# Inverse transform along h in a four-layer spectral kernel: products split by the parity of the frequency

## The reference

```python
x: (2, 64, 64, 384) float32; 8 blocks of 48 channels
# layers 0, 2 and 3 (scale of the transforms differs)
xf = rfft2(x, axes=(1, 2))                        # h, w -> 64 x 33 frequencies
o1r = relu(xr @ w1[0] - xi @ w1[1] + b1[0])       # block diagonal, 48 x 48
o1i = relu(xi @ w1[0] + xr @ w1[1] + b1[1])
o2r = o1r @ w2[0] - o1i @ w2[1] + b2[0]
o2i = o1i @ w2[0] + o1r @ w2[1] + b2[1]
x = irfft2(softshrink(o2r) + 1j * softshrink(o2i)) + x
# layer 1: the same with a Hartley transform over b, h, w and c,
# and mixes of the transform and the flipped input
x = dht(softshrink(mix(dht(x), flip(x)))) / size + x
```

## Time and profile before

| | |
|---|---|
| median of 3 runs | 995.19 us (990.65 to 997.57) |
| the profiled execution | 993.3 us, span 991.3 us |
| TensorE busy | 916.0 us, 92% |
| VectorE busy | 577.1 us, 58% |
| ScalarE busy | 475.8 us, 48% |
| granted clock of TensorE, mean | 0.976 |
| traffic of DMAs | 184.41 MB, mean 186 GB/s |

### The profile page before, as it was taken

One profiled execution on the slowest core, in us unless ns is written; L12 is line 12 of the kernel. 1 busy time (PEld: TensorE's weight loads), 2 busy tenths in 40 slices (PEclk: granted clock), 3 DMA queues, 4 the chain that ended last, 5 costly groups with the idle time before them and its releaser, 6 DMA issues.

```text
span 991.3 us, 14302 instructions
## 1 busy us (share of the span) xinstructions
PE 916.0 (92%) x5168; PEld 460.3 (46%) x5168; DVE 577.1 (58%) x869; ACT 475.8 (48%) x757; POOL 81.1 (8%) x157
## 2 busy tenths in 40 slices
PE   2799999999999988999999999999999999999933
PEld 1555555665676655444444434444444444444411
DVE  1255555455454765787775676666666666666511
ACT  2455444444545424434343445565655656666521
POOL 3011111011111110000000101000000000000001
PEclk8899999999999999999999999999999999999986
DMA  9879699469648979856143443343654474554463
GB/s 283 324 206 298 202 282 366 150 180 283 248 136 269 260 237 277 210 138 164 48 114 95 112 127 108 108 123 113 213 170 129 153 247 134 161 156 153 142 192 128
DMA packets 95703, 184.41 MB, mean 186 GB/s; under 512 B 13007, under 2 KB 73769, under 8 KB 93842
## 3 DMA queue, kind: packets, MB, share of 16 engines
q1 hardware_dynamic: 85490, 143.65, 48.0%
q0 software_dynamic: 9696, 39.56, 12.4%
q10 hardware_dynamic: 448, 0.30, 0.1%
HBM read 104.32 MB, written 79.14 MB: 185 GB/s over the span
## 4 chain that ended last, share of the span: by engine, by line
PE 82%; DMA 9%; SPq 2%; DVE 2%; ACT 2%; issue 1%; POOL 0%; ACTq 0%; DVEq 0%
PE psum L948 17%; PE psum L957 16%; PE psum L987 8%; PE psum L1041 6%; PE psum L1065 6%; PE psum L1025 6%; DMA RG<-rows_along_h 6%; PE psum L936 5%; PE psum L967 5%; PE psum L998 4%; PE psum L1052 3%; PE psum L913 3%; PE psum L1014 2%; DMA rows_along_h<-RD 1%; SPq L611 1%
## 5 line engine op out<-in xcount | busy, mean ns | idle before, releaser
L1374 DVE SCALAR_TENSOR_TENSOR RA<-psum,RA 112x896 f32<-112x896 f32 (+1 forms) x120 | 124.1, 1035 | 206.3 <-ACT RA L1222 205.9
L1222 ACT ACTIVATE RA<-psum,small 112x896 f32<-112x896 f32 (+1 forms) x120 | 115.7, 964 | 94.7 <-PE psum L957 94.7
L957 PE MATMUL psum<-RA,RW 112*64 112x448 f32 (+1 forms) x640 | 131.1, 531 | 1.4 <-ACT RA L1213 1.4
L1213 ACT ACTIVATE RA<-psum,RW 112x448 f32<-112x448 f32 (+1 forms) x160 | 89.2, 609 | 80.0 <-PE psum L948 80.0
L1334 DVE COPY RD<-psum 128x672 f32<-128x672 f32 (+2 forms) x122 | 69.5, 571 | 58.3 <-PE psum L987 56.8
L987 PE MATMUL psum<-RD,const 128*128 128x384 f32 (+1 forms) x304 | 98.3, 445 | 3.7 <-DVE RD L1334 2.7
L1207 ACT ACTIVATE RA<-psum 128x384 f32<-128x384 f32 (+2 forms) x72 | 50.6, 702 | 78.9 <-PE psum L936 52.6
L936 PE MATMUL psum<-const,RX 128*112 128x128 f32 x528 | 68.5, 282 | 17.1 <-DMA RX<-rows_along_w 17.1
L1359 DVE TENSOR_TENSOR RX<-RX,RA 112x768 f32<-112x768 f32 (+2 forms) x80 | 80.8, 1011 | 2.5
L1207 ACT ACTIVATE RD<-psum 128x384 f32<-128x384 f32 (+2 forms) x122 | 64.0, 525 | 32.9 <-PE psum L987 30.9
L936 PEld LDWEIGHTS psum<-const,RX 128*112 128x112 f32 x528 | 61.2, 180 | 35.7 <-issue 34.9
(11 more groups left out here) (103 smaller groups left out, 1070.1 us busy)
## 6 DMA issues: line engine op xcount, KB each, us to landing
RG<-rows_along_h SPq DMA_DIRECT2D x7, 3072.0 KB, 11.5
RX<-x SPq DMA_DIRECT2D x16, 768.0 KB, 8.6
rows_along_w<-RX SPq DMA_DIRECT2D x54, 224.0 KB, 5.1
rows_along_h<-RD SPq DMA_DIRECT2D x84, 144.0 KB, 3.3
rows_along_h<-RD SPq DMA_DIRECT2D x56, 168.0 KB, 2.9
out<-RA POOLq DMA_DIRECT2D x12, 768.0 KB, 4.0
RX<-rows_along_w SPq DMA_DIRECT2D x12, 672.0 KB, 6.5
spectrum<-RA POOLq DMA_DIRECT2D x48, 168.0 KB, 4.7
```

Of the source, the lines that this page charges most:

```text
L957: mm = nc.tensor.matmul(bank[b * HALF:(b + 1) * HALF, a * BANK:a * BANK + nk * H], w4[layer][0:ROWS, g, b, a], hidden(slot)[0:ROWS, b * N: ...
L1213: done = nc.scalar.activation(hidden(slot)[0:ROWS, b * N:b * N + nk * H], banks(key)[0:ROWS, b, 0:nk * H], ACT.Relu, bias=bias[layer][0:RO ...
L1222: nc.scalar.activation(dst, src, ACT.Relu, bias=minus_lambda_l0 if key[0] == "S4" else minus_lambda).then_inc(act_emptied, 1)
L1374: nc.vector.scalar_tensor_tensor(out=dst, in0=src, scalar=LAMBDA / 64 if key[0] == "S4" else LAMBDA, in1=dst, op0=ALU.add, op1=ALU.min).th ...
```

## The change

The rows of the h frequencies are held by parity in all tables and modes: 32 even frequencies first, then 32 odd. In `s5` each parity is a product of its own, with 64 rows and 64 output partitions (32 values of h, real and imaginary part), and the columns of a group are taken in two sets of four, one for each half of the output partitions (`set_columns`). So a unit is up to four products of 64x64. Bank 0 holds the even part, bank 1 the odd part. ScalarE copies the odd part to a new tile `odd_part`; VectorE waits for that and writes even + odd (h below 32) and even - odd (h from 32) to `turned`. A group's store is eight DMAs in place of four. In the last two groups ScalarE issues half of the stores, and the load of group 3 of the last pass comes one round later, behind the store of the last group. The rest follows from the order of rows: the views of the mixes, adds and folds have blocks of 32 in place of 64, and the output is stored in contiguous halves.

```diff
+SET = 4
-def bank_columns(e, part, half):
-    c0, c1 = columns_of(e)
-    lo, hi = ((0, 4), (4, c1 - c0))[part]
-    mid = lo + (hi - lo + 1) // 2
-    return ((lo, mid), (mid, hi))[half]
+def set_columns(e, part, half):
+    lo, hi = columns_of(e)
+    first = SET * half + 2 * part
+    return first, min(first + 2, SET * (half + 1), hi - lo)
...
+    by_parity = np.concatenate([a * H + np.arange(e, H, 2) for e in range(2) for a in range(2)])
...
+        odd_part = sb("odd_part", 2 * PASS_C)
...
             def store_turned(e):
                 lo, hi = columns_of(e)
-                for x in range(4):
-                    sp.dma_start(rows_along_h[group_of(e)[0], x, lo:hi].rearrange("k h c -> h k c"),
-                                 turned(e)[x * HP:(x + 1) * HP]).then_inc(turned_stored[e % TURN_SLOTS], 16)
+                for half in range(2):
+                    cols = range(lo + SET * half, min(lo + SET * (half + 1), hi))
+                    for x in range(4):
+                        sp.dma_start(rows_along_h[group_of(e)[0], x, cols.start:cols.stop].rearrange("k h c -> h k c"),
+                                     turned_rows(e, half, x % 2)[:, x // 2, 0:len(cols)]
+                                     ).then_inc(turned_stored[e % TURN_SLOTS], 16)
...
-                        store_spread(ALL_GROUPS + e, range(4) if e < ALL_GROUPS - 1 else range(2))
+                        for a in range(2 if e < ALL_GROUPS - 2 else 1):
+                            for j in range(2):
+                                for dst, src in spread_stores(ALL_GROUPS + e, a, j):
+                                    sp.dma_start(dst, src).then_inc(turned_stored[(ALL_GROUPS + e) % TURN_SLOTS], 16)
...
                 for q in range(PASS_GROUPS - 1):
-                    if r == min(10 * (PASSES - 1) + 7 + 2 * q, C_ROUNDS - 1):
+                    if r == (10 * (PASSES - 1) + 7 + 2 * q if q < PASS_GROUPS - 2 else C_ROUNDS - 1):
                         load_spread(LAST_PASS + q)
...
-                src = src.rearrange("p (k a h) -> p k a h", a=2, h=H)
+                src = src.rearrange("p (k a h) -> p k a h", a=2, h=HP)
...
+                d = D(first + e)
+                packed = e % PASS_GROUPS == 0
                 for half in range(2):
-                    lo, hi = bank_columns(e, part, half)
...
+                    lo, hi = set_columns(e, part, half)
+                    for parity in range(2):
+                        rows = slice(parity * HALF, (parity + 1) * HALF)
+                        dst = bank[half * HALF:(half + 1) * HALF, parity * BANK:parity * BANK + (hi - lo) * PASS_C
+                                   ].rearrange("p (k c) -> p k c", c=PASS_C)
+                        if packed and lo == 0:
+                            nc.tensor.matmul(dst[:, 0], matrix[rows, HALF:2 * HALF], d[rows, 0], start=True, stop=False)
+                            nc.tensor.matmul(dst[:, 0], matrix[rows, 2 * HALF:3 * HALF], d[rows, 1], start=False, stop=True)
+                            mm = nc.tensor.matmul(dst[:, 1:], matrix[rows, 0:HALF], d[rows, 2:hi + 1], start=True, stop=True)
+                        elif hi > lo:
+                            mm = nc.tensor.matmul(dst, matrix[rows, 0:HALF], d[rows, lo + packed:hi + packed],
+                                                  start=True, stop=True)
...
+        def wait_odd_part_free(eng, key):
+            stage, e, part = key
+            if part == 1:
+                eng.wait_ge(vec_emptied, plan.vec[stage, e, 0])
+            elif e > 0:
+                eng.wait_ge(vec_emptied, plan.vec[stage, e - 1, 1])
...
-                    wait_turn_free(act, at + key[1])
+                    wait_odd_part_free(act, key)
                     wait_filled(act, key)
-                    copy(*s5_views(key, 0, at)).then_inc(act_emptied, 1)
+                    _, _, odd, room = s5_views(key, at)
+                    copy(room, odd).then_inc(act_emptied, 1)
+                    if e >= 2 * ALL_GROUPS - 2 and key[2] == 1:
                         for part in range(2):
+                            act.wait_ge(vec_emptied, plan.vec["5C", key[1], part])
+                        for j in range(2):
+                            for dst, src in spread_stores(e, 1, j):
+                                act.dma_start(dst, src).then_inc(turned_stored[e % TURN_SLOTS], 16)
...
-                nc.vector.tensor_tensor(zr[:, :, 1:H], re[:, :, 1:H], re[:, :, H - 1:0:-1], ALU.add)
-                nc.vector.tensor_tensor(zi[:, :, 1:H], im[:, :, 1:H], im[:, :, H - 1:0:-1], ALU.subtract)
+                nc.vector.tensor_tensor(zr[:, :, 1:HP], re[:, 0, :, 1:HP], re[:, 0, :, HP - 1:0:-1], ALU.add)
+                nc.vector.tensor_tensor(zi[:, :, 1:HP], im[:, 0, :, 1:HP], im[:, 0, :, HP - 1:0:-1], ALU.subtract)
+                nc.vector.tensor_tensor(zr_odd, re[:, 1], re[:, 1, :, ::-1], ALU.add)
+                nc.vector.tensor_tensor(zi_odd, im[:, 1], im[:, 1, :, ::-1], ALU.subtract)
...
-                    wait_filled(vec, key)
-                    copy(*s5_views(key, 1, at)).then_inc(vec_emptied, 1)
+                    vec.wait_ge(act_emptied, plan.act[key])
+                    dst, even, _, odd = s5_views(key, at)
+                    nc.vector.tensor_tensor(dst[0], even, odd, ALU.add)
+                    nc.vector.tensor_tensor(dst[1], even, odd, ALU.subtract).then_inc(vec_emptied, 1)
```

101 lines of the change are left out of this document (46 added, 55 removed).

## The result

The changed kernel takes 999.96 us (median of 20 runs, 993.44 to 1005.99) and the kernel before 995.09 us (20 runs, 990.65 to 1002.37): ratio 1.0038, 95% interval 1.002 to 1.0056. The forecast was 972 us (963 to 984). The profiled execution took 997.33 us, its span is 995.5 us and its mean granted clock 0.954 (before: 991.3 us and 0.976).

What follows compares the result with a forecast made beforehand. TensorE was taken to bound the kernel (82% of the chain of waits). Savings of 26.1 - 2.4 - 1.4 - 1.0 + 2.1 = 23.4 us from 995.2 gave 971.8, rounded to 972 us (range 963 to 984).

Steps and rivals of the forecast that it cites:

- TensorE's products: The `s5` products, 80 units: from 100.8 to 74.7 us over 8 passes, so TensorE saves 26.1 us.
- Quartets and pairs: `s5` units of four or two 64x64 products: 0.80 us for four, 0.82 taken for two, start to start.
- The packed unit: `s5` unit with three 192-column products and one of 384 per parity: from 1.82 to 2.08 us, dearer by 0.26.
- Rival A: `s5`: array quarters work apart in the unit of mixed widths too (1.12 us), small charges halved: 962 us; chance 0.13.
- Evictions and folds (2.4): VectorE's second shrink of a round comes late in some 8 rounds with a fold, 0.3 us each: 2.4 us (0 to 5).
- rival B: `s5` evictions: ScalarE's copy, then two VectorE operations hold PSUM and set the pace; 19.8 us go: 992 us; chance 0.12.
- Short blocks: Operands of mixes and adds in blocks of 32 instead of 64 elements: cost taken as 0.
- Rival D: Mixes and adds: blocks of 32 cost TensorE or VectorE 5%: 982 us; chance 0.11.
- Transfers and SP's queue: Stores go from 4 to 8 issues: 1.4 us returned as first-stage gather wait, 1 us for SP elsewhere (0 to 10).
- Rival C: SP's queue, first stage: extra issues at 4.0 us each make loads and stores late, 45 us left over: 1015; chance 0.06.
- The end: Last load behind the stores gains 4.1 us, ScalarE's store issues give 2.0 back: net gain 2.1 us (-2 to 4).

Runs made afterwards that it cites:

- the change with three mends: Changed kernel with four stores a group, constant products thrown away ahead of five gathers, and group 18's stores left to SP: 976.76 us, 0.9821.

## Why the prediction was wrong

**TensorE's products: right, and too low.** Quartets and pairs take 0.79 to 0.81 us as said. The packed unit takes 1.55 us, not 2.08: the row of the second parity's first product stands at 707.86, ahead of the third of the first parity (708.18). My value took a product to start only behind the start of the one ahead, and here one starts 0.32 us before it; the measured unit lies between that and my 1.12 for quarters that are wholly apart. By the same sum the saving is 100.8 - 8 x (1.55 + 0.82 + 4 x 0.80 + 2 x 1.62) = 30.3 us; I had 26.1. Rival A had a part of the mechanism, and its price was lost with the rest. The two rules that I weighed, of the Trainium skill, TensorEngine Tiling (Array Packing), Key Properties (independent tiles), and of the Trainium skill, TensorE: Matmul & The Clock Gate, Part 3, The mechanism (products start and end in program order), would give 1.12 and 2.08 us; the trace agrees with neither. The starts at 707.86 and 708.18 are not in program order.

**Evictions and folds (2.4): not refuted.** VectorE's idle time ahead of the shrink went from 2.74 to 1.73 us, and over the whole kernel its idle time ahead of shrinks from 205.9 to 132.7: room was used, none ran out. VectorE's busy time rose by 48.5 us (577.1 to 625.6); I had 44 or more in the sum, 50 to 60 as a sign. (the earlier trace rows show 554 ns for the form that I priced at 548, which is 1 us over the 160 operations.) TensorE's list of waits names no shrink, and its longest wait for an eviction outside the end is 3.2 us where the kernel before has 2.7. The eviction's form alone cost 0 to 6 us in the kernel before. By the two together rival B falls; what of the 2.4 us was spent isn't resolved.

**Short blocks: 0, as taken.** The mixes cost the same (1.76 and 1.55 us for units of 448 and 384 columns, as in the earlier trace rows), and so do VectorE's adds (1092 and 958 ns for 896 and 768 columns in both kernels) and its shrinks (1089 and 955 ns, before 1088 and 954). Rival D falls.

**Transfers and SP's queue: the step that failed.** I wrote that the load "is issued by its round and lasts a fixed time" and charged 1.4 us there and 1 us elsewhere, up to 10. Measured by the number of issues, it is 13 us. The fixed time was right, or nearly: the first gather landed 15.4 us behind its issue before and 14.4 after, the third 11.8 and 11.0. What was wrong is the issue, and that I looked at one gather only. The load isn't issued when TensorE reaches its round. SP works off eight stores where it had four, and then waits for landings:

```profile
141.10 6.42 SPq L636 DMA_DIRECT2D rows_along_h<-RD  x8
```

```profile
141.28 4.10 SPq L640 DMA_DIRECT2D rows_by_part<-RD  x4
```

The first line is the changed kernel's, the second that of four stores. The stores to `rows_along_w` stand behind them in the queue. The last of these lands at 156.08 (153.60 with four), and SP, idle since 152.1, issues a load of these rows and, at 156.62 (154.14), the gather. The third gather is issued 0.1 us behind the landing of its group's last store, at 312.28 (311.27 before, 307.25 with four stores). The moment of one issue is known roughly: with eight stores and the same code up to there, four profiles have the first gather at 154.5 to 157.4, with four stores three have it at 153.8 to 154.4; the third is at 307.4 to 312.3 and at 300.6 to 307.3. So the first gather came only 0.7 us earlier than before although TensorE had gained 4.7 us, and 3.05 us of the 4.7 came back as wait, not the 1.4 of the three units between. The waits at 257, 320 and 402 grew too. In the last stage I had said that the wait "stays as it is"; it grew from 2.51 to 3.60 us at 720, 0.8 of it because the transfer took 12.0 us and not 11.2. Rival C named this mechanism and its place, at 0.06. Its price of 45 us was too high, and its point of decision (a store three rounds late) wrong: the gathers were late by far less.

**The clock: absent from the sum.** The kernel before had waits of 2.51 and 2.34 us in the last stage behind which the clock stayed at its full level, and I took that as given. In the changed kernel five waits for transfers, of 2.1 to 4.5 us, were each followed by 3.4 to 10.2 us at half, some 15 us in all. The run with the extra products shows it as a cause: 12.3 us come back, with 13.8 us of useless work put in. That fits the sum: the products cover about 13 us of wait at their five places and take 13.8, so what came back is the clock, by the estimate 13.4 us (half of the 30.6 us of low clock there, less the waits in it). Which waits it follows isn't settled by these runs: with four stores the clock fell behind one of 1.94 us, in the kernel before not behind one of 2.51. The Trainium skill (TensorE: Matmul & The Clock Gate, HAM oscillation) describes a kernel whose waits for loads made the clock fall again and again; the trace agrees that such a wait can cost twice (4.45 us idle, then 10.2 us at half clock), and I had not counted it.

**The end: wrong sign.** I took +2.1 us (-2 to 4). The order of loads did what it should: the last load is issued 4.2 us behind the last eviction (959.05 to 963.29), not 10.2. But ScalarE's four issues took 3.37 us, not 1.8, and all of the delay fell on TensorE, where I had counted 2.0: the last `5C` products waited 4.0 us more and then ran at half clock, 1.3 us more. From the last transposes to the last transforms it became 3.3 us longer, not 2.1 shorter. With the group's stores back on SP this stretch is 1.1 us shorter than before, and the kernel 6.4 us faster (interval some 3 to 10).

In sum: forecast -23.4, measured +3.8 (0.38% of 995) for the change and -17.8 for the change with three mends. What separates these 17.8 from the products' 30 isn't settled to the microsecond: there are 13.8 us of products of constants, of which about 6 fill waits that would stand at these five places (the version without them is at -14.6), and the longer waits of 0.1 to 0.6 us in the first stage.

## What to carry to other kernels

When a change shortens the bottleneck's work, list every transfer that it waits for, and ask of each what sets its *issue*: if that is a landing or a queue and not the bottleneck engine, the saved time returns as wait. Count the issues that a new layout adds, in the queue that also carries the large loads; four small stores more a group cost here some 40% of what the products saved (13 of 30 us), and a layout in which a store spans 64 partitions gets them back as long as the large gather stays whole. And price each new wait on TensorE with the slow stretch behind it: where a wait can't be avoided, a few products of constants are cheap, but only there: beside four stores they gained 0.3%, within noise, and in the kernel before they lost 0.7%.

## What the runs showed of the hardware

- The same pieces (768 bytes) and the same bytes in eight transfers in place of four: 1.4% in the kernel before, 1.3% in the changed one. Four issues took 1.79 us of SP's queue near the end and 2.79 at 154.67; eight took 18.79 us where transfers were full.
- The shape of a gather: 3 MB as 128 rows landed in 11.5 us in the median; as two transfers with an outermost dimension of 2 in some 90 us, at 53 GB/s and a fifth of the transfer engines.
- Four issues on ScalarE's queue took 3.37 us, and four on SP's at the same time 3.26; ScalarE's next four took 1.83. So an issue's time varied alike on both queues, from 0.45 to 0.84 us here, and on ScalarE its copies stood behind it.
- From issue to landing the first gather took 13.0 to 15.5 us in fourteen runs, with four stores issued behind it or eight; later ones took 9.9 to 13.2 us, once 14.9.
- Products of constants ahead of a wait kept the clock at its full level through it: 93 records against 38 in the same 10 us.
